# Maxima split on GpSimd, float32 transposes, two heads per quadrant in PV, first scores a slot ahead, evened slots, and the residual added in PSUM, in a fused attention and expert kernel

## The reference

```python
xn = _layernorm(x)
# attention, 16 heads of width 8, k and v from a latent of width 32
q = xn @ Wq + bq;  latent = xn @ Wl + bl;  k = latent @ Wk + bk;  v = latent @ Wv + bv
attn = softmax(einsum('bihd,bjhd->bhij', q, k) * SCALE)
a = einsum('bhij,bjhd->bihd', attn, v) @ Wo + bo
# experts, 8 heads: batch-normed queries against 2 x 32 unit keys, the best 4 of each
s0, s1 = q0 . k0, q1 . k1                  # 32 scores each, per token and head
ts0, ti0 = top_k(s0, 4);  ts1, ti1 = top_k(s1, 4)
comb_s = ts0[:, None] + ts1[None, :];  comb_i = ti0 * 32 + ti1
w = softmax(top_k(comb_s, 16));  idx = comb_i at those places      # 128 experts
eh = gelu(expert_down[idx] . xn);  f = sum(expert_up[idx] * eh * w)
out = x + a + f
```

## Time and profile before

| | |
|---|---|
| time, median of 3 runs | 461.19 us (456.23 to 469.43) |
| the profiled execution's own time | 458.13 us |
| span of that execution, first to last instruction | 456.2 us |
| mean granted clock of TensorE | 0.929 of full speed |
| opening, up to the first negm | 0 to 57 us |
| slots 0 to 7 | 57 to 107 us |
| one batch in the undisturbed middle | 20.48 us |
| after the last negm | 417 to 456 us |

### The profile page before, as it was taken

The page is one execution under the profiler, slowest core; times in us unless marked ns, Lnnn a source line. Parts: engine busy times, 40 slices in busy tenths (PEclk is TensorE's granted clock), DMA queues, the critical chain, the costliest instruction groups (busy, mean ns, idle before and its releaser), DMA issues.

```text
span 456.2 us, 10109 instructions
## 1 busy us (share of the span) xinstructions
PE 357.8 (78%) x3276; PEld 219.6 (48%) x3276; DVE 402.0 (88%) x1494; ACT 254.6 (56%) x387; POOL 275.8 (60%) x493
## 2 busy tenths in 40 slices
PE   3887698765787879697978769697969788786975
PEld 3443454422354546464645446464636455454544
DVE  5678489999979899999999999999999898998541
ACT  4556367653656557464656557565656464564650
POOL 3011237673588495957668595957668494959550
PEclk9989789875689899999999999999999898999897
DMA  7203924442841204050412223050504220000000
GB/s 204 59 0 88 129 67 135 129 114 57 104 74 14 66 8 73 11 83 3 84 31 53 60 26 84 2 84 2 82 28 58 57 29 14 3 13 1 27 12 12
DMA packets 46080, 24.88 MB, mean 55 GB/s; under 512 B 5644, under 2 KB 45900, under 8 KB 46028
## 3 DMA queue, kind: packets, MB, share of 16 engines
q1 hardware_dynamic: 46028, 24.24, 26.9%
HBM read 15.57 MB, written 8.39 MB: 53 GB/s over the span
## 4 chain that ended last, share of the span: by engine, by line
DVE 39%; issue 15%; POOL 14%; PE 10%; POOLq 1%; DMA 1%; SPq 0%; ACT 0%; DVEq 0%
DVE negm L856 12%; DVE r_sb L889 6%; DVE top L880 6%; DVE mpart L840 4%; PE bank L624 3%; DVE mpart L838 3%; POOL prod L1035 3%; POOL prod L1027 2%; DVE parts L699 2%; PE SI L520 2%; PE bank L640 2%; POOL z_sb L977 1%; POOL rank L997 1%; DVE ysb L829 1%; POOL cmp L987 1%
## 5 line engine op out<-in xcount | busy, mean ns | idle before, releaser
L413 ACT ACTIVATE Eb<-SJ 128x1024 f32<-128x1024 f32 x128 | 131.1, 1024 | 55.5 <-PE SJ L580 52.3
L856 DVE TENSOR_REDUCE negm<-SI 128x4 f32<-128x1024 f32 x128 | 153.7, 1209 | 9.3 <-PE SI L520 8.7
L600 PE MATMUL bank<-Eb,vhat 128*32 128x256 f32 x1024 | 72.0, 401 | 0.0
L1027 POOL TENSOR_TENSOR prod<-r_sb,a 128x1024 f32<-128x1024 f32 x31 | 59.5, 1941 | 0.0
L520 PE MATMUL SI<-KS,QS 48*128 48x256 bf16 x512 | 53.3, 289 | 6.7 <-DVE negm L856 3.8
L960 POOL COPY top<-top 128x32 f32<-128x32 f32 x32 | 6.7, 209 | 84.3 <-DVE top L880 84.3
L580 PE MATMUL SJ<-QS,KS 50*128 50x256 bf16 x512 | 51.4, 280 | 5.1 <-ACT Eb L413 4.2
L938 POOL TENSOR_TENSOR Eb<-Eb,parts 128x512 f32<-128x512 f32 x16 | 20.0, 1266 | 58.5 <-ACT parts L303 58.5
L880 DVE MAX8 top<-s_sb 128x8 f32<-128x32 f32 x512 | 50.4, 176 | 5.1 <-ACT s_sb L387 5.1
L889 DVE MATCH_REPLACE8 r_sb<-top,s_sb 128x36 f32<-128x36 f32 x256 | 42.7, 179 | 0.0
L624 PE MATMUL bank<-kblk,fqT 128*128 128x256 f32 x128 | 40.8, 446 | 0.3
(11 more groups left out here) (147 smaller groups left out, 691.7 us busy)
## 6 DMA issues: line engine op xcount, KB each, us to landing
qk_parts<-parts SPq DMA_DIRECT2D x48, 128.0 KB, 2.4
QS<-qk_parts SPq DMA_DIRECT2D x32, 96.0 KB
KS<-qk_parts SPq DMA_DIRECT2D x32, 96.0 KB
x_sb<-L_attn_x SPq DMA_DIRECT2D x8, 256.0 KB, 3.8
QS<-qk_parts SPq DMA_DIRECT2D x32, 64.0 KB
KS<-qk_parts SPq DMA_DIRECT2D x32, 64.0 KB
out<-ysb SPq DMA_DIRECT2D x16, 128.0 KB, 3.8
QS<-qk_parts SPq DMA_DIRECT2D x32, 32.0 KB
```

The source lines that it names most:

```text
L413: A(Eb[:, n % 4, :], SJ[:, :], ACT.Exp).then_inc(s["ex"], 1)
L600: last = mm(psO[32 * c:32 * c + 32, (g % 2) * S:(g % 2 + 1) * S], vhat[:, v0:v0 + 32], Eb[:, (2 * g + c // 2) % 4, e0:e0 + S], start=(t == ...
L856: V.tensor_reduce(negm[:, bb % 2, :, :, pr].rearrange("p e t -> p (e t)"), si_buffer(slot)[:, :].rearrange("p (t j) -> p t j", j=S), axis= ...
L1027: TT(prod[:, t, :, :, :], r_sb[:, hs, 0:NK].unsqueeze(2).to_broadcast([P, FH, TOP, NK]), a0[:, hs, :].unsqueeze(3).to_broadcast([P, FH, TO ...
```

## The change

1. **Maxima split on GpSimd.** The two instructions for `mpart` move from DVE (k = 0 of the next batch) to POOL (k = 7 of the same batch), and the layout of `negm` is that of the transposed result. Two DMAs instead of four bring `mT` to `QS`.
2. **float32 transposes.** Where a float32 matmul with an identity transposed (L455, L563, L658), `transpose` is used. `wt` becomes eight transposing matmuls per token tile that add up in PSUM (k = 3 and k = 4), so that POOL's addition of head halves (L1035) falls away, and the remainder is added per token tile.
3. **PV of two heads per quadrant.** `vhat` gets zeros between the heads, so that weights of 18 columns put a head in the first or the second 9 rows of a quadrant. Two groups add into one PSUM half, which ACT copies to `Osb` every fourth slot, two copies per batch instead of four. The selection matmuls (L651) become four plain transposes. The heads' columns of Wq, Wk, bq, bk are permuted before launch.
4. **First scores a slot ahead.** From slot 10 on PE issues `si(slot + 1)` behind PV of slot, in place of `si(slot)` at its start.
5. **Evened slots.** DVE does `negm` first in every slot. MATCH_REPLACE8 goes in four quarters (k = 4 to 7), the masked product (L900) to k = 0 of the next batch, `den` and `dinv` stay in k = 6, the division (L819, L821) goes from k = 6 to k = 5, POOL's `top4` and ranking one slot earlier, its `prod` to k = 0, 1.
6. **Residual in PSUM.** The output matmuls get a third operand pair, identity times `x_sb`, per token tile; ACT instead of DVE copies the result to `ysb`, in k = 0.
7. The zeros and ones of `vhat`, now twice as large, are written by POOL (5/8) and DVE (3/8) at the start, and the bfloat16 identity is a view of the float32 one, without the cast L750.

The core of the diff:

```diff
 # ACT
-                    A(Osb[:, g % 4, :], psO[:, (g % 2) * S:(g % 2 + 1) * S], ACT.Copy).then_inc(s["o_ev"], 1)
+                m = slot - LAG - 6
+                if m >= 0 and m % 4 == 0 and m // 4 < 2 * B:
+                    q = m // 4
+                    act.wait_ge(s["pv"], 2 * q + 2)
...
+                    A(Osb[:, q % 2, :], psO[:, (q % 2) * S:(q % 2 + 1) * S], ACT.Copy).then_inc(s["o_ev"], 1)
...
+                by = (slot - LAG - 13) // 8
+                if k == 0 and 0 <= by < B:
+                    act.wait_ge(s["y"], by + 1)
...
+                    A(ysb[:, by % 2, :, :].rearrange("p t d -> p (t d)"), psM[:, 0:S], ACT.Copy).then_inc(s["fin"], 1)
...
+                if k == 0 and 0 <= b < B:
+                    act.wait_ge(s["mt"], b + 1)
...
+                    A(mT[:, :], psM[0:2 * H, 0:S], ACT.Copy).then_inc(s["mt_ev"], 1)
 # PE
-                if slot < NPAIR * B:
+                if slot <= FIRST2:
                     si(slot)
...
-                            h = 2 * (g % 4) + c // 2 + NPAIR * (c % 2)
+                            h = 8 * (q % 2) + 2 * c + u
+                            v0 = VC + (BT * b + t) * VT + 2 * VC * h - VC * u
-                            last = mm(psO[32 * c:32 * c + 32, (g % 2) * S:(g % 2 + 1) * S], vhat[:, v0:v0 + 32],
+                            last = mm(psO[32 * c:32 * c + 2 * VC, (q % 2) * S:(q % 2 + 1) * S], vhat[:, v0:v0 + 2 * VC],
...
+                if FIRST2 <= slot < NPAIR * B - 1:
+                    si(slot + 1)
...
-                        for h in range(FH // 2):
-                            last = mm(psM[:, t * P:(t + 1) * P], prod[:, t, h, :, :].rearrange("p i j -> p (i j)"), ident,
+                    for h in range(FH):
+                        last = mm(psM[:, t * P:(t + 1) * P], prod[:, t, h, :, :].rearrange("p i j -> p (i j)"), ident,
+                                  start=(h == 0), stop=(h == FH - 1), is_transpose=True)
...
-                        for g in range(4):
-                            last = mm(ct[:, :, 2 * g * VC:2 * (g + 1) * VC], Osb[:, g, t * P:(t + 1) * P],
-                                      sel, start=True, stop=True)
+                        for q in range(2):
+                            last = turn(psM[:, (2 * t + q) * P:(2 * t + q + 1) * P], Osb[:, q, t * P:(t + 1) * P], ident)
...
-                        last = mm(psM[:, t * D:(t + 1) * D], wgT[:, t * P:(t + 1) * P], up_sb[:, :], start=False, stop=True)
+                        mm(psM[:, t * D:(t + 1) * D], wgT[:, t * P:(t + 1) * P], up_sb[:, :], start=False, stop=False)
+                        last = mm(psM[:, t * D:(t + 1) * D], ident, x_sb[:, BT * b + t, :], start=False, stop=True)
 # DVE, k = 0: gone
-                    V.tensor_tensor(ysb[:, b % 2, :, :], psM[:, 0:S].rearrange("p (t d) -> p t d", t=BT),
-                                    x_sb[:, BT * b:BT * (b + 1), :], ALU.add).then_inc(s["fin"], 1)
-                    V.tensor_copy(mpart[:, :, :, 0, :], src).then_inc(s["mh"], 1)
...
-                    V.tensor_tensor(mpart[:, :, :, 1, :], src, mpart[:, :, :, 0, :], ALU.subtract).then_inc(s["ms"], 1)
 # POOL
+                bm = slot // 8
+                if k == 7 and bm < B:
+                    pool.wait_ge(s["mx"], NPAIR * (bm + 1))
...
+                    V.tensor_copy(mpart[:, :, :, 0, :], most).then_inc(s["mh"], 1)
...
+                    TT(mpart[:, :, :, 1, :], most, mpart[:, :, :, 0, :], ALU.subtract).then_inc(s["ms"], 1)
+                b = slot // 8 - 2
+                if k in (0, 1) and 0 <= b < B and not (b == B - 1 and k == 1):
+                    pool.wait_ge(s["fa"], b + 1)
+                    pool.wait_ge(s["es"], b + 1)
...
-                        TT(prod[:, :, 0:FH // 2, :, :].rearrange("p t h i j -> p t (h i j)"),
-                           prod[:, :, 0:FH // 2, :, :].rearrange("p t h i j -> p t (h i j)"),
-                           prod[:, :, FH // 2:FH, :, :].rearrange("p t h i j -> p t (h i j)"), ALU.add).then_inc(s["pr"], 1)
+                    lastx = prod[:, t, :, TOP - 1, NK - 1]
+                    TT(lastx, lastx, p0r[:, 2, hs], ALU.add).then_inc(s["pr"], 1)
 # SP
-                    for part in range(2):
-                        sp.dma_start(QS[r0:r0 + 1, b % RING, :, :], mT[src:src + NPAIR, :]).then_inc(s["mrow"], 16)
+                    sp.dma_start(QS[r0:r0 + 2, b % RING, :, :], mT[H * e:H * (e + 1), :]).then_inc(s["mrow"], 16)
```

More of the change, by code:

```diff
@@ L40, in constants @@
     c[p, C_ID + p] = 1.0
-    for col in range(4):
-        for r in range(9):
-            c[32 * col + r, C_SEL + 18 * (col % 2) + 9 * (col // 2) + r] = 1.0
     c[:, C_AVG:C_AVG + P] = (p[:, None] % 32 == p[None, :] % 32) / 8.0
@@ L63, in program @@
     VC = DH + 1
+    VT = 2 * H * VC
     FH, FQ = 8, 32
@@ L424, in _ @@
             mm = nc.tensor.matmul
+            turn = nc.tensor.transpose
             def project_qk(c):
@@ L454, in _ @@
                     for t in range(TC):
-                        last = mm(psX[c % 2][:, t * P:(t + 1) * P], xn_sb[:, c % 2, t, :], ident, start=True, stop=True)
+                        last = turn(psX[c % 2][:, t * P:(t + 1) * P], xn_sb[:, c % 2, t, :], ident)
                     last.then_inc(s["xT"], 1)
@@ L562, in _ @@
                     for t in range(NC // 2):
-                        last = mm(psN[:, t * P:(t + 1) * P], rn_t[:, t * P:(t + 1) * P], ident, start=True, stop=True)
+                        last = turn(psN[:, t * P:(t + 1) * P], rn_t[:, t * P:(t + 1) * P], ident)
                     last.then_inc(s["rnT"], 1)
@@ L657, in _ @@
                     for t in range(BT):
-                        last = mm(psM[:, t * P:(t + 1) * P], on[:, t, :], ident, start=True, stop=True)
+                        last = turn(psM[:, t * P:(t + 1) * P], on[:, t, :], ident)
                     last.then_inc(s["onp"], 1)
@@ L881, in _ @@
                     last.then_inc(s["t8"], 1)
-                if k in (4, 5) and 0 <= b < B:
-                    t = k - 4
-                    dve.wait_ge(s["t4"], 2 * b + t + 1)
-                    if b >= 1:
-                        dve.wait_ge(s["pr"], 4 * b)
-                    for h in range(FH * t, FH * (t + 1)):
-                        last = V.match_replace(r_sb[:, h, :], top4[:, h, :], s_sb[:, h, 1, :], NEG)
-                    last.then_inc(s["mr"], 1)
                 if k == 6 and 0 <= b < B:
                     dve.wait_ge(s["ze"], b + 1)
-                    dve.wait_ge(s["mr"], 2 * b + 2)
                     if b >= 1:
@@ L899, in _ @@
                                     axis=AX, op=ALU.add).then_inc(s["fd"], 1)
+                    dve.wait_ge(s["fd"], b + 1)
+                    V.reciprocal(dinv[:, :, :], den[:, :, :]).then_inc(s["fe"], 1)
+                if k in (4, 5, 6, 7) and 0 <= b < B:
+                    quarter = k - 4
+                    t = quarter // 2
+                    dve.wait_ge(s["t4"], 2 * b + t + 1)
+                    if b >= 1:
+                        dve.wait_ge(s["pr"], 4 * b - 2 * (1 - t))
+                    for h in range(NH // 4 * quarter, NH // 4 * (quarter + 1)):
+                        last = V.match_replace(r_sb[:, h, :], top4[:, h, :], s_sb[:, h, 1, :], NEG)
+                    last.then_inc(s["mr"], 1)
+                b = slot // 8 - 2
+                if k == 0 and 0 <= b < B:
+                    dve.wait_ge(s["ze"], b + 1)
+                    dve.wait_ge(s["mr"], 4 * b + 4)
                     V.scalar_tensor_tensor(r_sb[:, :, 0:NK], r_sb[:, :, 0:NK], NEG, z_sb[:, :, 0:NK],
                                            ALU.is_equal, ALU.mult).then_inc(s["es"], 1)
[L902 to L904 removed]
+                if k == 1 and b == B - 1:
                     dve.wait_ge(s["fa"], B)
                     dve.wait_ge(s["es"], B)
[L908 to L909 removed]
+                    dve.wait_ge(s["wt"], 2 * b)
                     V.tensor_tensor(prod[:, 1, :, :, :], r_sb[:, FH:NH, 0:NK].unsqueeze(2).to_broadcast([P, FH, TOP, NK]),
@@ L1017, in _ @@
                     TT(p0r[:, 2, :], p0r[:, 1, :], dinv[:, :, 0], ALU.mult).then_inc(s["rest"], 1)
-                if k in (6, 7) and 0 <= b < B and not (b == B - 1 and k == 7):
-                    t = k - 6
+                bm = slot // 8
+                if k == 7 and bm < B:
+                    pool.wait_ge(s["mx"], NPAIR * (bm + 1))
+                    if bm >= 1:
+                        pool.wait_ge(s["mt"], bm)
+                    most = negm[:, bm % 2, :, :, :]
+                    V.tensor_copy(mpart[:, :, :, 0, :], most).then_inc(s["mh"], 1)
+                    pool.wait_ge(s["mh"], bm + 1)
+                    TT(mpart[:, :, :, 1, :], most, mpart[:, :, :, 0, :], ALU.subtract).then_inc(s["ms"], 1)
+                b = slot // 8 - 2
+                if k in (0, 1) and 0 <= b < B and not (b == B - 1 and k == 1):
+                    t = k
                     pool.wait_ge(s["fa"], b + 1)
@@ L1051 @@
     for name in NAMES:
```

(3 more changed lines are left out.)

186 lines of the change are left out of this document (83 added, 103 removed).

## The result

The changed kernel takes 399.39 us (median of 4 runs, 396.66 to 402.81) beside 461.36 (median of 4, 456.23 to 469.43) for the kernel before: a ratio of 0.867, 95% interval 0.856 to 0.878. The profiled execution took 396.66 us, with a span of 395.0. The forecast was 399.2. It was reckoned from a profiled execution, and between profiled executions the gain is 61.5 us, where 58.9 was forecast.

What follows compares the result with a forecast made beforehand. DVE was taken as the bound. Thirteen batches falling from 20.86 to 17.3 us give 46.3 us; with 4.7, 3 and 4.9 that is 58.9, from 458.13 to 399.2 us. Range: 392 to 407 us, chance 0.62.

Steps and rivals of the forecast that it cites:

- DVE's sum: DVE in a middle batch: `ysb` and two `mpart` steps removed, 3.63 us, leaving a floor of 16.85 us.
- The coupling: Waits between engines in a batch, for `wgT` and the maxima rows: 0.45 us added, 17.3 us a batch.
- the landing of the maxima rows: Second scores of k = 3 wait for the maxima rows' DMA, due within 0.1 us of PE's arrival.
- PE: PE's busy time in a middle batch falls from 16.60 to 15.3 us, with one instruction a transpose.
- Rival 1: PE becomes the bound, by two instructions a transpose or idle gaps: 420 us; chance 0.22 shared with the maxima's way.
- POOL and ACT: Busy time in a middle batch: POOL falls from 14.73 to 12.8 us, ACT from 11.97 to below 12.
- the 1.2 that was feared: `mpart` on POOL in k = 7, behind the ranking, comes 1.2 us late after the batch's last `negm`.
- Slots 0 to 7: At slots 7 and 8 POOL's bias addition stands behind `mpart`, so `mt` comes earlier: 4.7 us gained.
- the term of 3 us: Slots 8 to 23, partly at 1.2 GHz: between 0 and 2 x 3.6 us gained, 3 taken.
- The end: After the last batch: savings on `mpart`, the last addition of halves and selection, less the residual: 4.9 us gained.
- DVE at its floor: Rival: all waits hidden in the batches, slots 8 to 23 and opening gain fully: 387 us; chance 0.10.
- PE's clock falling: Rival: PE falls to 1.2 GHz, 532 us if throughout; chance 0.02 for clock partly down, 428 to 449 us.

Runs made afterwards that it cites:

- 10: The changed kernel with first scores in their own slot again and `wgT` behind k = 4's quarter of MATCH_REPLACE8: 393.00 us, ratio 0.863.
- Experiment 2: The changed kernel with both `mpart` operations back on DVE at the start of k = 0, POOL's `prod` left in its new place: 407.72 us, ratio 0.896.
- 6: The changed kernel with the residual added by DVE in k = 0, without PE's third operand pair and ACT's copy: 404.66 us, ratio 0.884.
- Experiment 7: The changed kernel with first scores at the start of their own slot again: 396.14 and 389.80 us in two runs, no ratio.
- experiment 5: The changed kernel with the 16 transposing matmuls of `wt` as plain float32 matmuls: 433.48 us, ratio 0.947.
- experiment 4: The changed kernel with POOL's bias addition ahead of `mpart` in slot 7: 405.62 us, ratio 0.891.
- 1: The changed kernel with `wgT` moved behind the quarter of MATCH_REPLACE8 in k = 4 on DVE: 395.57 us, ratio 0.869.
- 12: The kernel before with float32 transposes alone, POOL's addition of halves kept: median 478.76 us of six runs, beside 460.37 for the kernel before.

## Why the prediction was right, and where it was not

**DVE's sum: right.** 20.48 - 3.63 = 16.85 was forecast. Busy time after is 16.86 us, and 10 ran at 16.85. Experiment 2 splits the 3.63: 3.0 us were waiting for POOL's running instruction, 0.3 the operations themselves, and 6 gives the 0.32 of `ysb`. The Trainium skill, in SBUF — State Buffer, section "Who interferes with whom", describes such an exclusive lock between DVE and GpSimd for casts that can take both of DVE's ports, and for operations with two inputs in SBUF; the 0.17 us of the cast beside an idle POOL and the 1.50 beside a busy one agree with it.

**The coupling: the term of 0.45 us was mis-sized, and its cause half seen.** The prediction put 0.2 us on `wgT` and 0.25 on the landing of the maxima rows, 17.3 us in all. The landing cost nothing. `wgT` waited 0.67 us, and with 0.08 of small gaps that makes 17.60. The forecast named the right instruction and the right queue, "behind second scores, PV and the next first scores", but took for granted that first scores a slot ahead are needed to absorb the unevenness. Experiment 7 shows that they cost more than they absorb here. In twelve batches that makes 3.6 us. The mean of 20.86 us before hid something too: not only the first batch but also the last ones before slot 120 took longer than 20.48 (20.88, 22.02 and 21.97 us, the latter two at a granted clock of 0.92). Of the 39.6 us gained there, 34.6 are the pace, 12 x 2.88, and 5.0 are these batches, which the kernel after doesn't have.

**PE: 16.03 us busy instead of 15.3**, clock 1.00, transposes one instruction of 0.125 us as taken. Experiment 10 has the same instructions in another order and is busy for 15.1 to 15.4 us, so some of the 16.03 is how overlapping matmuls are counted; how much isn't shown. Rival 1 with two instructions a transpose is refuted by the pace in the timeline, and experiment 5 shows what it would have meant for `wt` alone, 19.5 us a batch.

**POOL and ACT: right.** POOL is busy for 12.92 us (12.8 forecast) and ACT for 11.32 (below 12). `mpart` takes 0.21 and 0.24 us, as bounded. It starts 0.1 us behind the last `negm` (222.92 + 1.22) and not the 1.2 that was feared, since POOL's ranking ends just then.

**Slots 0 to 7: 4.7 us forecast, 9.8 gained.** The cause was right, the order of the bias addition (7.7 us by experiment 4, some 8 by 2). The size was read off the wrong engine: PE's idle 4.70 us before `mt`. But the `negm` of slot 8 doesn't wait for `mt`; it stands behind L699 on DVE. From one `negm` to the next (slots 7 and 8) it was 9.55 us before (97.44 to 106.99) and is 1.79 after (95.00 to 96.79): the 8.18 us of L699 became 0.67. DVE's queue gave 7.8 us. The other 2.0 lie in slots 0 to 6, and 1.83 of them are two waits of DVE for first scores (1.27 us in slot 1, 0.56 in slot 6) that the trace of after doesn't have, at a granted clock of 0.91 before and 0.99 after. No edit need be behind them: the control, the same program as after, has 0.74 us of such a wait in slot 1 and takes 41.40 us for slots 0 to 7.

**Slots 8 to 23: 6.6 us forecast, 2.3 gained; here the term of 3 us was mis-sized.** The row holds the `mpart` and `ysb` of slot 24, 3.6 us on DVE. For the 3 us beside them there was nothing to take: in the kernel before, the casts of slots 8 and 16 took 0.17 us and 0.18 (at 125.94), beside a POOL that was idle or in operations of 0.4 us and less, and no `ysb` comes before slot 24. And what DVE sheds here doesn't all shorten the stage. In slots 16 to 23 of the kernel after DVE is busy for 17.24 of 21.76 us, PE for 19.00 at a granted clock of 0.83, and DVE waits 4.5 us in five places, for first scores, key scores and `wt`. The prediction had said that PE often sets the pace there, but took half of DVE's steps all the same.

**The end: 9.2 us for 4.9.** From the start of the last `negm` to the last `prod` on POOL it was 22.2 us (415.74 to 437.93 in the trace of before) and is 17.3 (363.72 to 381.06): 4.9 us, where the sum had 2.8 for `mpart` and nothing for a ranking one slot earlier. From there to `wt` 1.7 us fell with the addition of halves (1.22 forecast), and from `wt` to `wgT` 0.5. From `wgT` to the last `ysb` it is 4.75 us for 6.94: selection and residual gave 2.2, where 1.0 was forecast. (The forecast's own terms for the end add up to 5.0, not 4.9.)

**The rivals.** DVE at its floor did not come in the changed kernel, but lies two changes of order away (10; 1 alone gives 16.95). PE's clock falling had 0.02. For the change as a whole that was right: clock 1.00 in every batch of the middle. With the transposes by themselves it did fall, in five executions of six (12). The prediction's reason why the whole should escape was that the waits for `mpart`, 45.6 us in all before, go. That fits the clock after, but no run separates it from the rest of the change: it is argued, not shown.
